# Two routed FFNs: slots of 256 rows of one expert, the first weights as the stationary operand

## What is computed

```python
def ffn(x, router_w, w1, w2):                 # 8 experts, hidden 512, 2 experts per token
    logits = einsum('btd,ed->bte', x, router_w)
    top_vals, top_idx = top_k(logits, 2)
    top_w = softmax(top_vals)
    h = square(relu(einsum('nd,edh->enh', xf, w1)))
    y = einsum('enh,ehd->end', h, w2)
    return sum over the two chosen experts of top_w * y
x = x + 0.5 * ffn(layernorm(x)); x = x + mamba2(layernorm(x)); x = x + 0.5 * ffn(layernorm(x))
```

## Time and profile before

| | us |
|---|---|
| median of three runs | 1248.7 |
| the profiled execution's own time | 1249.26 |
| its span, first to last instruction | 1247.5 |
| first FFN: front and routing, about | 0 to 107 |
| first FFN: main loop, about | 107 to 368 |
| Mamba layer, about | 375 to 910 |
| second FFN: routing, about | 910 to 947 |
| second FFN: main loop and end, about | 947 to 1247 |

### The profile page before, as it was taken

How to read it: one execution, slowest core, us unless ns; L and a number is a source line. 1 busy time by engine, 2 the same in 40 slices (tenths; PEclk the granted TensorE clock), 3 DMA queues, 4 the chain that set the end, 5 groups by cost and what they waited for, 6 DMA issues and landing times. The chain is left out here.

```text
span 1247.5 us, 21987 instructions
## 1 busy us (share of the span) xinstructions
PE 1012.6 (81%) x6624; PEld 860.8 (69%) x6656; DVE 738.8 (59%) x1614; ACT 606.3 (49%) x1568; POOL 596.8 (48%) x612
## 2 busy tenths in 40 slices
PE   3746999999974788988888888888737999999960
PEld 3745999999963566766666666666526999999950
DVE  6975444444436868678788777765365444444437
ACT  1323555555532455465655656565424555555530
POOL 6922555555522236354545454547503555555520
PEclk9998999999995689799999999999858999999985
DMA  7872222322313101011111110000062223322339
GB/s 229 278 301 75 73 77 77 96 77 77 79 42 107 50 27 46 22 54 37 59 43 43 43 39 18 18 18 26 30 278 63 91 96 93 97 91 95 92 115 324
DMA packets 73259, 112.22 MB, mean 90 GB/s; under 512 B 10680, under 2 KB 60352, under 8 KB 71872
## 3 DMA queue, kind: packets, MB, share of 16 engines
q1 hardware_dynamic: 48704, 60.48, 14.6%
q0 software_dynamic: 13824, 37.77, 9.5%
q10 hardware_dynamic: 10624, 12.58, 3.0%
HBM read 66.76 MB, written 44.04 MB: 89 GB/s over the span
## 5 line engine op out<-in xcount | busy, mean ns | idle before, releaser
L427 POOL DMA_INDIRECT ys_d<-xs,row_of x144 | 142.5, 989 | 194.6 <-DVE xs L811 188.9
L491 ACT ACTIVATE hs<-pH 128x512 f32<-128x512 f32 x144 | 86.1, 598 | 229.5 <-PE pH L613 229.5
L422 POOL DMA_INDIRECT xs<-xn_d,token_of x144 | 140.0, 972 | 114.2 <-DVE token_of L785 70.9
L800 DVE TENSOR_TENSOR xl<-pT,xh 128x256 fp32r<-128x256 f32 x144 | 61.1, 425 | 221.3 <-ACT xh L504 221.0
L805 DVE TENSOR_TENSOR h2l<-hs,h2h 128x512 fp32r<-128x512 f32 x144 | 99.8, 693 | 77.1 <-ACT h2h L499 76.9
L1615 DVE SCALAR_TENSOR_TENSOR acc<-bank,cwh,acc 128x511 f32<-128x511 f32 (+2 forms) x120 | 89.6, 747 | 43.6 <-ACT acc L1224 40.8
L633 PE MATMUL pY<-w2h,h2h 128*128 x576 | 103.3, 301 | 0.5 <-DVE h2l L805 0.4
L1128 POOL TENSOR_TENSOR yv<-yv,sz 128x512 f32<-128x512 f32 x32 | 40.7, 1271 | 116.7 <-DVE yv L1657 113.5
L613 PE MATMUL pH<-w1h,xh 128*128 x288 | 92.6, 403 | 1.8 <-DVE xl L800 1.1
L613 PE MATMUL pH<-w1l,xh 128*128 x288 | 92.1, 402 | 0.0
L633 PE MATMUL pY<-w2h,h2l 128*128 x576 | 91.1, 280 | 0.0
(11 more groups left out here) (255 smaller groups left out, 2581.0 us busy)
## 6 DMA issues: line engine op xcount, KB each, us to landing
m_yg<-ys_d SPq DMA_DIRECT2D x64, 128.0 KB, 2.2
xs<-ys_d SPq DMA_DIRECT2D x12, 512.0 KB, 6.6
wst<-in_L_ffn_w_dram ACTq DMA_DIRECT2D x8, 512.0 KB, 4.5
xs<-in_L_attn_x_dram SPq DMA_DIRECT2D x8, 512.0 KB, 6.3
hs<-in_L_ffn_w_dram ACTq DMA_DIRECT2D x8, 512.0 KB, 4.8
xn_d<-xs SPq DMA_DIRECT2D x8, 512.0 KB, 3.3
lo_d<-w1l SPq DMA_DIRECT2D x1, 4096.0 KB, 11.8
lo_d<-w2l SPq DMA_DIRECT2D x1, 4096.0 KB, 21.4
```

Of the source, the lines that this page charges most:

```text
L422: pool.indirect_dma_start(out=xg[:, t % NX, :], out_offset=None, in_=xn_d, in_offset=bass.IndirectOffsetOnAxis(ap=token_of[:, t:t + 1], ax ...
L427: pool.indirect_dma_start(out=ys_d, out_offset=bass.IndirectOffsetOnAxis(ap=row_of[:, t:t + 1], axis=0), in_=y[:, t % NX, :], in_offset=No ...
L491: act.activation(r[:, u, :], pH[u][:, :], ACT.Relu).then_inc(relu_done.sem, 1)
L800: dve.tensor_tensor(xl[:, u, :, :], src, xh[:, u, :, :].bitcast(F32), ALU.subtract).then_inc(g_split.sem, 1)
```

## The change

A slot is now up to 256 rows of one expert. NP = 32 pair slots hold two tiles each and are followed by 8 single slots (one per expert at most) of one tile: NJ = 40 slots, still NT = 72 tiles. The routing gives each expert its full pairs, a left-over of two tiles goes to a pair while pairs are free, and the rest to singles.

- **up**: the stationary operand is a 128 by 128 piece of w1, the moving one is x, 256 columns, in a single slot too (half of them unused). h comes out already turned, so `turn_h` is gone. h takes four PSUM banks (two per slot in two halves).
- **w1** is no longer kept. For each slot SP reads the expert's number, loads the raw 512 KB from the input (`load_w1`, four buffers, two and more slots ahead), ACT rounds it (`round_w`) and DVE subtracts (`split_w`).
- **w2** alone is split in the front, 8 units, and both its parts stay in SBUF. `lo_d`, its writes and its reads are gone.
- ACT now does relu and the rounded square of h in two halves (`round_h`), and the copy of y for a slot; DVE does the exact square, and the low parts of w1, x and h.
- Pool's loop is as it was, tile by tile. `gather(t)` waits for the slot of tile t-8, `scatter(t)` for `y_copied` of its slot.
- The routing's chain has more operations for the two kinds of slots; `expert_i` is found ahead of the inversion, and PE waits for `experts_known` ahead of the first `turn_x`.
- The early loads stand in SP's loop at slots 8 and 22, and the early splits at slots between 6 and 27.

The diff, cut:

```diff
-    NT = (TOP * TOK + E * (P - 1)) // P
-    NT += -NT % NX
+    NP = TOP * TOK // (2 * P)
+    NJ = NP + E
+    NT = 2 * NP + E
...
-        NW = 2 * E
+        NW = E
...
+            def load_w1(j):
+                if j >= NRAW:
+                    sp.wait_ge(w1_lo.sem, w1_lo.done(j - NRAW))
+                elif first:
+                    sp.wait_ge(w_lo.sem, w_lo.done(NW - NRAW + j))
+                at = sp.value_load(expert_i[0:1, 1, j:j + 1], min_val=0, max_val=(E - 1) * D)
...
             def gather(t):
                 if t >= NX:
-                    pool.wait_ge(g_T.sem, g_T.done(t - NX))
+                    pool.wait_ge(g_T.sem, g_T.done(slot_of(t - NX)))
...
             def scatter(t):
-                pool.wait_ge(y_copied.sem, y_copied.done(t))
+                pool.wait_ge(y_copied.sem, y_copied.done(slot_of(t)))
...
+            def copy_y(j):
+                act.wait_ge(y_ready.sem, y_ready.done(j))
...
+            for j in range(NJ):
+                if j + 1 < NJ:
+                    round_h(j + 1, 0)
+                if j + 3 < NJ:
+                    round_w(j + 3)
+                if j + 1 < NJ:
+                    round_h(j + 1, 1)
+                if j + 3 < NJ:
+                    round_x(j + 3)
...
+                copy_y(j)
...
+            def turn_x(j):
+                pe.wait_ge(g_split.sem, g_split.done(j - 2))
+                for u, t in enumerate(tiles_of(j)):
+                    pe.wait_ge(gathered[t % NX].sem, gathered[t % NX].done(t // NX))
...
+            def up(j):
+                u = j % 2
+                pe.wait_ge(g_split.sem, g_split.done(j))
+                pe.wait_ge(w1_lo.sem, w1_lo.done(j))
+                for b in range(2):
+                    pe.wait_ge(relu_done.sem, relu_done.done(2 * (j - 2) + b))
+                    for q in range(2):
+                        n = 0
+                        for w, a in ((w1h, xh), (w1h, xl), (w1l, xh)):
+                            for k in range(KD):
+                                at = k * HID + (2 * b + q) * P
+                                last = pe.matmul(pH[u][b][:, q * 2 * P:(q + 1) * 2 * P], w[:, u, at:at + P], a[:, u, k, :], start=(n == 0), stop=(n == 3 * KD - 1))
+                                n += 1
+                    last.then_inc(h_ready.sem, 1)
...
+            for j in range(NJ):
+                at = expert_columns(j)
+                if j + 1 < NJ:
+                    up(j + 1)
+                if j + 3 < NJ:
+                    turn_x(j + 3)
+                down(j, at)
...
+            for j in range(NJ):
+                if j + 1 < NJ:
+                    square(j + 1, 0)
+                    split_h(j + 1, 0)
+                    square(j + 1, 1)
+                if j + 3 < NJ:
+                    split_w(j + 3)
+                if j + 1 < NJ:
+                    split_h(j + 1, 1)
+                if j + 3 < NJ:
+                    split_x(j + 3)
```

More of the change, by code:

```diff
@@ L362, in _ @@
                     store(rounds - 1, h)
[L363 to L371, removed]
+            sp.wait_ge(experts_known, 1)
+            for j in range(NJ):
+                load_w1(j)
+                if first and j == EARLY_LOAD[0]:
+                    sp.dma_start(early["wo"][:, :, :], early["w_out"].rearrange("(k p) n -> p k n", p=P)).then_inc(out_loaded, 16)
+                    sp.dma_start(early["nw"][:, :], early["norm_w"].rearrange("(k p) -> p k", p=P), allow_slow_non_contiguous=True).then_inc(out_loaded, 16)
+                if first and j in EARLY_LOAD:
+                    k = EARLY_LOAD.index(j)
+                    if k > 0:
+                        sp.wait_ge(early_split, k)
                     sp.dma_start(early["raw"][:, :], early["w_in"][k * P:(k + 1) * P, :]).then_inc(early_loaded, 16)
+                if out is not None and j % EG == 0 and 2 * EG <= j:
+                    n = j // EG - 2
+                    sp.wait_ge(y_copied.sem, y_copied.done(n * EG))
+                    sp.dma_start(res[:, n * EG:(n + 1) * EG, :], tiles(x, n * EG * P)).then_inc(res_loaded, 16)
             if out is not None:
[L374 to L377, removed]
                 for u in range(NX):
@@ L487, in _ @@
                 last.then_inc(oh_col.sem, 1)
[L489 to L513, removed]
+            def round_w(j):
+                act.wait_ge(w_loaded[j % NRAW], 16 * (j // NRAW + 1 + (NW // NRAW if first else 0)))
+                act.wait_ge(h_ready.sem, up_done(j - 2))
+                act.activation(w1h[:, j % 2, :], wraw[:, j % NRAW, :], ACT.Copy).then_inc(w1_hi.sem, 1)
@@ L514, in early_high @@
+            def copy_y(j):
+                act.wait_ge(y_ready.sem, y_ready.done(j))
+                n = len(tiles_of(j))
+                for t in tiles_of(j):
+                    if t >= NX:
+                        act.wait_ge(scattered[t % NX].sem, scattered[t % NX].done(t // NX - 1))
+                t = tiles_of(j)[0] % NX
+                act.activation(y[:, t:t + n, :], pY[j % 2][:, 0:n * D].rearrange("p (n d) -> p n d", n=n), ACT.Copy).then_inc(y_copied.sem, 1)
             def early_high(k):
@@ L518, in early_high @@
                 act.activation(wih[:, k, DIN:], raw[:, DIN:], ACT.Copy).then_inc(early_hi, 1)
[L520 to L528, removed]
+            round_w(0)
+            round_w(1)
+            round_x(0)
+            round_x(1)
+            round_h(0, 0)
+            round_w(2)
+            round_h(0, 1)
+            round_x(2)
+            for j in range(NJ):
[7 more added lines that the diff above has]
+                    round_x(j + 3)
+                if first and j in EARLY_HI:
+                    early_high(EARLY_HI.index(j))
+                copy_y(j)
             if out is not None:
@@ L592, in _ @@
             pe.transpose(pY[0][:, 0:NT], inv[0:NT, :], ident[0:NT, 0:NT]).then_inc(invT_ready, 1)
-            def expert_columns(t):
-                return pe.value_load(expert_i[0:1, t:t + 1], min_val=0, max_val=(E - 1) * WCOLS)
-            def turn_x(t):
-                pe.wait_ge(gathered[t % NX].sem, gathered[t % NX].done(t // NX))
-                for k in range(KD):
-                    last = pe.transpose(pT[t % 2][:, k * P:(k + 1) * P], xg[:, t % NX, k * P:(k + 1) * P], ident[:, :])
-                last.then_inc(g_T.sem, 1)
@@ L618, in turn_h, with expert_columns @@
[L618 to L635 removed]
+            def expert_columns(j):
+                return pe.value_load(expert_i[0:1, 0, j:j + 1], min_val=0, max_val=(E - 1) * WCOLS)
@@ new lines, in down @@
+            def down(j, at):
+                pe.wait_ge(h_split.sem, h_split.done(2 * j + 1))
+                pe.wait_ge(y_copied.sem, y_copied.done(j - 2))
+                hi, lo = w2h[:, bass.ds(at, WCOLS)], w2l[:, bass.ds(at, WCOLS)]
+                for u in range(len(tiles_of(j))):
+                    n = 0
+                    for a, w in ((h2h, hi), (h2h, lo), (h2l, hi)):
+                        for k in range(KH):
+                            last = pe.matmul(pY[j % 2][:, u * D:(u + 1) * D], a[:, j % 2, k, u * P:(u + 1) * P], w[:, k * D:(k + 1) * D],
+                                             start=(n == 0), stop=(n == 3 * KH - 1))
+                            n += 1
@@ L661, in _ @@
         @block.vector
         def _(dve):
-            for s in (w_hi, st_chain, mv_done, var_done, norm_done, oh_hi, oh_lo, g_split, h2_split, y_copied):
+            for s in (w_hi, st_chain, mv_done, var_done, norm_done, oh_hi, oh_lo, w1_lo, g_split, sq_done, h_split):
                 s.open(dve)
@@ new lines, in _ @@
+            link(dve.tensor_copy(smalli[:, 1, :], total))
+            link(dve.tensor_scalar(smalli[:, 2, :], smalli[:, 0, :], P.bit_length() - 1, None, ALU.logical_shift_right))
+            link(dve.tensor_scalar(smalli[:, 3, :], smalli[:, 1, :], P.bit_length(), None, ALU.logical_shift_right))
+            link(dve.tensor_copy(small[:, 0:2, :], smalli[:, 2:4, :]))
+            every, full, rest, big, in_pairs, in_singles, takes = (small[:, n, :] for n in (0, 1, 2, 3, 4, 5, 12))
+            gate_of = small[:, 6:8, :].rearrange("p a e -> p (a e)")
@@ new lines, in _ @@
+            ends, starts = small[:, 8:10, :], small[:, 10:12, :]
+            link(dve.memset(gate_of, 1.0))
+            link(dve.memset(small[:, 7, 0:1], 0.0))
+            link(dve.scalar_tensor_tensor(rest, full, -2.0, every, ALU.mult, ALU.add))
+            link(dve.tensor_scalar(big, rest, float(TOP), None, ALU.is_equal))
+            link(dve.tensor_copy(small[:, 2 + 12, :], full))
+            link(dve.tensor_copy(small[:, 3 + 12, :], big))
+            link(dve.tensor_tensor_scan(small[:, 16:18, :].rearrange("p a e -> p (a e)"), gate_of, small[:, 14:16, :].rearrange("p a e -> p (a e)"), 0.0, ALU.mult, ALU.add))
```

283 lines of the change are left out of this document (136 added, 147 removed).

## The result

| | us |
|---|---|
| before, median (1247.84 to 1252.97) | 1249.53 |
| after, median (1453.27 to 1457.75) | 1455.55 |
| after by before, 95% interval | 1.1646 (1.1622 to 1.167) |
| predicted, with its range | 1343 (1315 to 1435) |

The change makes the kernel 206 us slower, 112 us more than predicted. The page of the changed kernel: span, busy time by engine, the clock in 40 slices, the group of the turns of x with the idle time before them, and the group of the gathers.

A forecast was written before the change was run, and what follows sets the result against it. PE's stream bounds the kernel now; after the change, late gathers stall it. From 1249.3 us, +94 for both loops, +9.6 routing and -10 front gave 1343 us, range 1315 to 1435.

The forecast's parts named there:

- The stall: At turn_x in pair slots, PE waits 2.36 us for a gather queued behind a scatter, 28 times per loop.
- Rival 1: At turn_x the gather isn't late and PE stays the bound: loops -20 and -18, 1210 us; chance 9%.
- The clock: In both FFN loops, no cost counted for a falling clock; down stays at 2.82 us.
- rival 2: The clock falls in every turn_x stall, 1.5 us each, 56 times: 84 us, 1427 us in all; chance 11%.
- The landing: In the loops, a gather takes 2.82 us from its start to PE's turn, bounds 2.38 to 4.76.
- The sum of a slot: A stalled pair slot takes 8.44 us from down to down: PE works 6.08 and stands 2.36.
- The loop's ends: Each FFN loop: 17 us from the second gather through the first down, 50.5 us after the 28 stalled slots.
- Front and routing: First FFN's front gets 10 us shorter; routing's added DVE operations cost 4.8 us per FFN, 9.6 together.
- Other engines: In the loop, ACT's 4.8 and DVE's 5.5 us per pair fit under 6.08; SP's w1 loads are hidden.

The follow-up runs named there:

- lead2: Changed kernel with the gathers of slot j+6 put ahead of the scatters of slot j in Pool's queue; 1226.01 us, 0.9803 of before.
- shift1: Changed kernel with every gather one place earlier in Pool's queue, gather(t+9) before scatter(t); 1243.3 us, 0.9933 of before.
- fill: Changed kernel with 20 unread matmuls of 256 columns on PE in each stalled slot, where it would stand; 1383.42 us, 1.1064 of before.
- noload: Changed kernel fetching only 8 columns of w1 per slot from the fifth slot on; 1450.63 us, 1.1602 of before.
- narrow: Changed kernel with DVE's square of h and split of w1 cut to 8 columns per row from the third slot; 1422.89 us, 1.1367 of before.

## Why the prediction was right, and where it was wrong

- **The stall: right.** Where PE stands, on what, and behind which scatter, was read from Pool's order alone, and lead2 and shift1 confirm it: moving the gather ahead of that scatter takes the stall away. Rival 1 took the opposite view and falls; its time was nearly reached only once the order was changed.
- **The clock: wrong, and the step that failed.** The forecast put the clock's cost at nothing: it kept down at 2.82 us and gave rival 2 only 11%, because 6.08 us of dense work lie between stalls, a gap of 1.54 us had kept the clock, and the front seemed to keep it in every step. Down took 4.29, with matmuls 0.21 apart, the prediction's own sign of rival 2. Two of its readings did not carry so low a chance. By its matmuls the front ran near the low level: the trace of the kernel before has no clock record for its first 92 us, where the table prints 1.00 all the same, and four turns from 30.25 to 31.16 stand 0.23 us apart, against 0.11 in the loop at full clock and 0.21 for turns of the same shape at 0.50 (two from 552.21 to 552.63). And the wait of 1.80 us was one of five of that length at L1419 in the Mamba layer: four were followed by 0.50 and one by 1.00. From the kernel before, PE in the front, then windows of 4 us behind two of these waits:

```profile
30.25 1.12 PE L551 MATMUL pT<-ident,xs 128*128 128x128 f32 x4 [1.89 <-DVE xs L690]
31.16 1.72 PE L559 MATMUL pY<-rwT,room 128*128 128x8 f32 x8
...
483.39:487.39 4.00, 4.00 (x28) 1.00 0.14 37
549.24:553.24 4.00, 4.00 (x17) 0.57 0.11 33
```

The forecast stall of 2.36 us was longer than all of these. The price of rival 2 was right: 1.5 us estimated, 1.43 measured by fill. Its sum with the measured landing, 1427 + 56 x 0.42 = 1451 us, comes within 5 us of the measured time; the stated range had room for rival 2, but not for both. The Trainium skill ("TensorE: Matmul & The Clock Gate", the part on HAM oscillation) describes bursts of matmuls, shorter than the transfer waits between them, of which each starts cold. The trace agrees in the cold start, at 0.50 for some 3 us behind the stalls, though here the bursts are longer than the waits.
- **The landing: mis-sized, from 2.82 to 3.24 us.** The prediction's bounds (2.38 to 4.76) held it, but for another reason than the traffic named there: a gather that starts while a DVE operation from SBUF to SBUF runs ends its issue 0.84 us behind that operation's end. At 227.80, L857 had 0.59 us left and the issue took 1.43 instead of 0.97; at 230.83, L847 had 1.14 left and it took 1.98. Over the gathers of the changed kernel that started so, 56 beside L857 and 64 beside L847, the median of these 0.84 us is the same. noload rules traffic out in these slots, and narrow brings 0.97 and 2.79 back. The gather of the earlier trace rows took 0.97 beside `split_x`, which started 0.04 us ahead of it but reads one of its operands from PSUM; so did the 119 gathers of the kernel before that started beside it, in the median. The Trainium skill ("SBUF — State Buffer", "Who interferes with whom" and the part on the two sides) has a port pair that VectorE and GpSimd share as a lock: an operation of VectorE with two SBUF inputs blocks one of GpSimd that reads SBUF, if it starts first. The trace agrees in this: the scatter of 229.54, which started before the square at 230.14, took its usual 0.99. The same section infers that a `tensor_tensor` does not stall GpSimd's writing of descriptors; the issues of 1.43 and 1.98 us differ from that, whichever part of the issue it is that was held.
- **The sum of a slot.** 8.44 + 0.42 (landing) + 1.43 (clock) = 10.29, against 10.24 measured. From the first copy on, the 28 stalled intervals of the first loop took 288.8 us, where 28 x 8.44 = 236.3 were forecast: 52.5 more. It is not quite 28 x 1.80 = 50.4, as the last two of them, at the change to singles, were longer (12.46 and 10.59). In the second loop they took 293.1, with 12.24 for the first and 12.48 and 11.38 for the last two. Together that is 109 of the 112 us.
- **The loop's ends.** From the second gather to the end of the first down it took 123.53 - 103.70 = 19.8 us, forecast 17.0 (its terms add up to 16.6): the third and fourth gathers were held beside `split_w` too (1.49 and 1.85 us of issue). The tail took 50.9, forecast 50.5.
- **Front and routing: right.** The last logits of the first FFN, and the end of its routing, from the timeline of the changed kernel:

```profile
60.99 0.18 ACT L479 ACTIVATE logits<-pY 128x8 f32<-128x8 f32 x1 [0.68 <-PE pY L589]
...
101.72 0.20 DVE L839 TENSOR_SCALAR token_of<-row_t 128x72 uint32<-128x72 uint32 x1
```

The logits come 10.5 us sooner than in the earlier trace rows (10 forecast). From DVE's first operation at 61.27 the routing takes 101.92 - 61.27 = 40.65 us, against 35.19 before: 5.5 more, where 4.8 was forecast. In the second FFN it takes 40.65 against 34.70, 5.9 more.
- **Other engines: right about ACT, DVE and SP.** Neither w1's loads nor its splits are waited for in the stalled slots. (DVE's 5.5 us do not follow from their pieces, which add up to 4.8; both lie below 6.08.) What was not costed is what DVE's new work does to Pool: in lead2 it lifts Pool's slot from 0.99 + 0.97 + 1.00 + 1.00 + 4 x 0.30 = 5.16 to 6.16 us.

What stays open is why the first stalled slot, with 3.02 us without a matmul, kept its clock. The slots of narrow that kept it are not scattered by chance: the granted clock over the 2.5 us from the turn's start is 0.53, 0.61, 0.68, 0.76, 0.84 and 1.00 at the six stalls that end at 177.28, 187.15, 197.03, 206.86, 216.71 and 226.50, and then the climb starts again. What sets this rhythm was not tried.

## What to carry to other kernels

When PE's work is grouped into larger units, regroup the queues that feed it as well: a gather written behind a scatter of the unit before turned a gain of 2% into a loss of 16%, and one place in the queue decided. Price a stall of PE as the stall plus what the low clock costs behind it, if waits of that length in the profile drop the clock at all; one row that kept it does not settle the matter, and a stretch without a clock record says nothing. Where GpSimd issues indirect transfers, see which VectorE operations with two inputs in SBUF run when they start, and how much of each is then left.

## What the runs showed of the hardware that was not expected

- Stalls of about 2.4 us, with some 6 us of dense matmuls between them, dropped the granted clock to 0.50 in nearly every period, which cost 1.43 us each; 20 matmuls that compute nothing, in the stall's place, made the kernel 72 us faster.
- The issue of an indirect gather, 0.97 us by itself, took 1.43 to 1.98 us when it started inside VectorE's `tensor_tensor` on SBUF, also without w1's traffic: it ended 0.84 us behind that operation. Scatters too: twelve that started inside L847, with 0.32 us of it left, took 1.17 in the median instead of 0.99.
- Matmuls of 128 columns, each with its own weight load, came 0.11 us apart, those of 256 columns 0.12.
